# Moving half blocks, row selections, mask slices and transposes to other steps of an image

## The reference

```python
om = conv(x, w_om, 3x3) + b_om             # 108 channels: 36 dy, 36 dx, 36 mask
py = h - 1 + ki + dy ; px = w - 1 + kj + dx  # per group (4), tap (9), pixel
v  = (bilinear sample of x at py, px, zero outside) * sigmoid(mask)
out = relu(einsum('ogck,bgckhw->bohw', w_dcn, v)) + x
```

## Time and profile before

| what | us |
|---|---|
| median of 3 runs | 207.06 |
| the runs | 206.66 to 207.31 |
| the profiled execution | 207.24 |
| its span, first to last instruction | 205.1 |
| busy in the span: PE / PEld | 180.4 / 127.2 |
| busy in the span: DVE / ACT / POOL | 161.3 / 106.3 / 86.2 |

### The profile page before, as it was taken

How to read it: one execution, slowest core, us unless ns; L and a number is a source line. 1 busy time by engine, 2 the same in 40 slices (tenths; PEclk the granted TensorE clock), 3 DMA queues, 4 the chain that set the end, 5 groups by cost and what they waited for, 6 DMA issues and landing times.

```text
span 205.1 us, 4582 instructions
## 1 busy us (share of the span) xinstructions
PE 180.4 (88%) x1806; PEld 127.2 (62%) x1806; DVE 161.3 (79%) x268; ACT 106.3 (52%) x199; POOL 86.2 (42%) x103
## 2 busy tenths in 40 slices
PE   0398997979899989999889999999969999998980
PEld 0234944644356544477578779639958789877870
DVE  0899778994768859887889779717999798899922
ACT  1146057500007784688748757836766687864000
POOL 8237952864013096504444344240661554442000
PEclk9999999999999999999999999999999999999999
DMA  6940000000130000010011000000002000000000
GB/s 189 327 33 2 3 0 0 3 0 0 29 77 19 20 27 9 25 36 3 9 36 25 0 3 0 3 0 3 9 25 70 20 2 16 0 16 2 19 0 21
DMA packets 8499, 5.54 MB, mean 27 GB/s; under 512 B 4887, under 2 KB 7461, under 8 KB 8473
## 3 DMA queue, kind: packets, MB, share of 16 engines
q1 hardware_dynamic: 8089, 4.25, 8.1%
q10 hardware_dynamic: 288, 0.89, 1.4%
q0 software_dynamic: 96, 0.06, 0.1%
HBM read 2.82 MB, written 0.52 MB: 16 GB/s over the span
## 4 chain that ended last, share of the span: by engine, by line
PE 66%; DVE 16%; ACT 6%; issue 4%; DMA 3%; POOL 2%; SPq 0%; DVEq 0%; ACTq 0%; POOLq 0%
PE ps L1254 20%; PE ps L1228 10%; PE ps L1148 10%; PE ps L1044 4%; PE ps L1165 3%; DVE smp_prod L777 3%; DMA x_parts<-in_x 3%; PE ps L1296 3%; PE ps L1302 3%; PE ps L1081 3%; PE ps L1213 2%; PE ps L1199 2%; DVE smp_prod L888 2%; PE ps L1182 2%; DVE windows_attention L873 1%
## 5 line engine op out<-in xcount | busy, mean ns | idle before, releaser
L888 DVE TENSOR_TENSOR smp_prod<-ps,hx_selx 128x768 f32<-128x768 f32 x72 | 67.5, 953 | 10.1 <-PE ps L1228 8.8
L1254 PE MATMUL ps<-smp_prod,windows_attention 128*64 128x192 f32 (+2 forms) x512 | 54.9, 336 | 0.0
L1254 PEld LDWEIGHTS ps<-smp_prod,windows_attention 128*64 128x64 f32 x512 | 40.1, 136 | 4.1 <-ACT windows_attention L575 0.3
L1228 PE MATMUL ps<-haty,by_rows 128*64 128x256 f16 x432 | 39.4, 275 | 2.0 <-DVE smp_prod L888 1.8
L451 POOL TENSOR_SCALAR disty<-disty 64x512 f32<-64x512 f32 (+1 forms) x23 | 13.5, 586 | 64.3 <-ACT haty L596 64.2
L1228 PEld LDWEIGHTS ps<-haty,by_rows 128*64 128x64 f16 x432 | 26.1, 109 | 9.7 <-DVE smp_prod L888 3.9
L604 ACT ACTIVATE hx_selx<-ps 128x512 f32<-128x512 f32 x36 | 21.3, 591 | 10.8 <-PE ps L1213 10.8
L458 POOL TENSOR_TENSOR haty<-disty,haty 64x512 f16<-64x512 f32 (+1 forms) x23 | 24.0, 1042 | 1.9
L1148 PE MATMUL ps<-conv_staged 128*108 128x512 f32 (+1 forms) x60 | 23.3, 521 | 0.7 <-ACT x_parts L568 0.7
L606 ACT ACTIVATE hx_selx<-hx_selx 128x512 f32<-128x512 f32 x36 | 22.7, 631 | 1.2
L591 ACT ACTIVATE disty<-ps 128x512 f32<-128x512 f32 (+1 forms) x24 | 12.5, 521 | 12.3 <-PE ps L1199 12.3
...
## 6 DMA issues: line engine op xcount, KB each, us to landing
...
```

The lines of the kernel that those rows point to most:

```text
L888: nc.vector.tensor_tensor(pairs, rows, cols.unsqueeze(1).to_broadcast([P, QUARTERS, HW]), ALU.mult).then_inc(s_mult, 1)
L1228: ins = nc.tensor.matmul(ps[h * C:(h + 1) * C, at:at + HW], by_matrix(a, QUARTERS - 1 - k)[:, h * C:(h + 1) * C], haty[i % 2][:, p * HW:(p ...
L1254: return nc.tensor.matmul(dst[:, at:at + strips * 3 * SP].rearrange("p (s k n) -> p s k n", k=3, n=SP), rows, sampled(i, ki, m, first, str ...
```

## The change

Half block (1,1) stays at step 0, (2,0) goes from step 1 to 2 and (2,1) from 2 to 3. The row selections go from steps 1, 3, 7 to 2, 6, 8, the mask slices from 0, 2, 6, 8 to 0, 3, 5, 7 (in image 0 from 4, 5, 6, 8 to 4, 5, 7, and in image 1 there are five instead of four). VectorE's last values of an image go from step 3 to 4. Images 1 and 2 transpose at steps 2, 3, 5 instead of 2, 3, 4, 5, and image 3 gets two groups, at steps 2 and 3; VectorE copies a group out of bank 4 in the same step and not in the next. The waits for copied groups ahead of blocks and `final` name other groups accordingly.

```diff
--- before.py
+++ after.py
@@ -64,9 +64,9 @@
 YW, YP = [HW, 2 * HW, 2 * HW], [0, 1, 3]
 MSLOT = 3 * BANK + 3 * HW
 
-MASKS = [{4: (0, 0), 5: (0, 1), 6: (0, 2), 8: (0, 3)}, {0: (0, 4), 2: (0, 5), 6: (1, 0), 8: (1, 1)},
-         {0: (1, 2), 2: (1, 3), 6: (1, 4), 8: (1, 5)}, {0: (2, 0), 2: (2, 1), 6: (2, 2), 8: (2, 3)},
-         {0: (2, 4), 2: (2, 5)}, {0: (3, 0), 2: (3, 1), 6: (3, 2), 8: (3, 3)}, {0: (3, 4), 2: (3, 5)}, {}]
+MASKS = [{4: (0, 0), 5: (0, 1), 7: (0, 2)}, {0: (0, 3), 1: (0, 4), 3: (0, 5), 5: (1, 0), 7: (1, 1)},
+         {0: (1, 2), 3: (1, 3), 5: (1, 4), 7: (1, 5)}, {0: (2, 0), 3: (2, 1), 5: (2, 2), 7: (2, 3)},
+         {0: (2, 4), 3: (2, 5)}, {0: (3, 0), 3: (3, 1), 5: (3, 2), 7: (3, 3)}, {0: (3, 4), 3: (3, 5)}, {}]
 
 
 PIECES = [(0, 0, HW), (0, HW, BANK), (1, 0, BANK), (2, 0, BANK), (3, 0, BANK)]
@@ -74,16 +74,16 @@
 CONV_BANK = [4, 0, 6, 6, 4]
 EARLY = 3
 PAIRS_AT = {(0, m): (EARLY + m, 4) for m in range(6)} | {
-    (1, 2): (9, 6), (1, 3): (10, 6), (1, 4): (11, 4), (1, 5): (12, 4),
-    (2, 2): (13, 6), (2, 3): (14, 6), (2, 4): (15, 4), (2, 5): (16, 4)}
+    (1, 2): (9, 6), (1, 3): (10, 6), (1, 5): (11, 4), (2, 2): (12, 6), (2, 3): (13, 6), (2, 5): (14, 4),
+    (3, 2): (15, 6), (3, 3): (16, 6)}
 PARTS_AT = {(0, m + 1): (2, m) for m in range(5)} | {(1, m + 2): (3, m) for m in range(5)} | {(4, m): (4, m) for m in range(5)}
 STAGE_AT = {(0, 0): 1, (0, 2): 2, (0, 7): 3}
 LAST_CONV = 3
 FAR = 5
 CHUNK, VALS, SLICES = 3, 3, 6
-SEL_Y = {1: 0, 3: 1, 7: 2}
+SEL_Y = {2: 0, 6: 1, 8: 2}
 BLOCKS = {6: (0, 0), 7: (0, 1), 8: (1, 0)}
-LATE = {0: (1, 1), 1: (2, 0), 2: (2, 1)}
+LATE = {0: (1, 1), 2: (2, 0), 3: (2, 1)}
 FINAL = 5
 
 
@@ -937,16 +937,17 @@
                         values(i, 0, it)
                     if m == 1 and i:
                         values(i - 1, 1, it)
-                    if m == 3 and i:
+                    if m == 4 and i:
                         values(i - 1, 2, it)
                     if m == FINAL + 1 and i:
                         accumulate(i - 1, it)
                         if isinstance(it, int):
                             finish(i - 1, 1)
                     if isinstance(it, int):
-                        if (i, m - 1) in PAIRS_AT:
-                            g, src = PAIRS_AT[i, m - 1]
-                            if g % 2:
+
+                        for at in (m - 1, m):
+                            g, src = PAIRS_AT.get((i, at), (0, 0))
+                            if g % 2 and (at == m) == (i > 0 and src == 4):
                                 window_out(g, it, src)
                         if (i, m) in PARTS_AT:
                             offset_part(*PARTS_AT[i, m])
@@ -1331,7 +1332,7 @@
                                          stop=True).then_inc(s_amaxT, 1)
                     if m in BLOCKS:
                         if i < 3 and m == 6 and isinstance(it, int):
-                            windows_out(8 + 4 * i, it)
+                            windows_out(8 + 3 * i, it)
                         if i == 0 and m == 8 and isinstance(it, int):
                             pe.wait_ge(s_omraw, 4)
                         if (i, m) == (LAST_CONV, 6) and isinstance(it, int):
@@ -1356,7 +1357,7 @@
                         spread_mask(*MASKS[i][m], it)
                     if (i, m) in PAIRS_AT and isinstance(it, int):
                         g, dst = PAIRS_AT[i, m]
-                        if i == 0 or m in (3, 5):
+                        if i == 0 or m == 3:
                             windows_out(g - 1, it)
                         else:
                             pe.wait_ge(s_vals, VALS * (i - 1) + (2 if m == 2 else 3))
@@ -1364,12 +1365,12 @@
                             pe.wait_ge(s_staged, {4: 2, 8: 3, 12: 4}[g])
                         windows(g, it, dst)
                     if m == FINAL and i:
-                        if i in (1, 2) and isinstance(it, int):
-                            windows_out(6 + 4 * i, it)
+                        if i in (1, 2, 3) and isinstance(it, int):
+                            windows_out(7 + 3 * i, it)
                         if i == FAR and isinstance(it, int):
                             pe.wait_ge(s_choice, 1)
                         final(i - 1, it)
-                for m in range(3):
+                for m in LATE:
                     block_of_products(B - 1, *LATE[m], it)
                 final(B - 1, it)
```

## The result

The changed kernel takes **204.23 us** (median of four runs, 203.85 to 204.55); the kernel before took 207.19 us beside it on the same chip (206.66 to 207.38). The ratio is 0.9855, with a 95% interval of 0.9833 to 0.9877: 2.96 us or 1.45% faster. The forecast was 205.0 us with a range of 203.4 to 206.8. The profiled execution took 204.55 us, its span 202.5 us, so a difference of spans (2.6 us) is what the two traces have to explain. Of the runs of the experiments one is left out of the medians and ratios as a slow one, over 1.5% above the fastest of its kernel (213.30 us, all but the half blocks).

A forecast was written before the change was run, and what follows sets the result against it. Late stretches were taken as bound by VectorE and TensorE together, neither filling them, stretch 3 by TensorE alone. Terms -1.5 +0.4 +0.1 -0.5 -0.6 = -2.1 us gave 205.0 us, range 203.4 to 206.8.

The forecast's parts named there:

- stretch 7: Last sampling-loop stretch, cut at final projections: alternating heavy and light steps removes TensorE waits; worked out 0.80 us gain, 0.6 taken.
- stretches 1 and 2: Sampling-loop stretches with transposes: fewer groups and no waits for VectorE copies, less 0.2 for mask slice 2; -1.5 us.
- stretch 3: TensorE-bound sampling-loop stretch: two transpose groups come (0.84 us), the 0.40 us wait at bank 7 goes; +0.4 us.
- stretches 4 and 5: Sampling-loop stretches: VectorE's work on the last offsets in image 4 stays, values come one step later; +0.1 us.
- stretch 6: Sampling-loop stretch like the last but with mask slices: the 0.64 us wait for bank 7 goes; -0.5 us.
- the sentence on the Trainium skill: GpSimd contends with two-SBUF-input VectorE instructions; moved chain keeps full speed, result copy loses its GpSimd neighbour; gains 0.8 us in stretch 7.
- alternation: Sampling-loop steps: light steps between heavy ones cut VectorE and TensorE waits; worked out on stretch 7, 0.80 us gain.
- Slice 2 at step 7: Mask slice 2 moves to one step before the values that read it; hidden if TensorE is late there, 0.2 us charged.
- (a): Rival, more gain than counted: VectorE's idle falls to 0.6 us in stretches 1, 2, 4 to 7; 203.5 us, chance 0.10.
- (b): Rival, waits only move: 0.2 us more before the final projection in seven images, 0.3 for slice 2; 206.7 us, chance 0.12.
- (c): Rival, second row selection's ScalarE and GpSimd chain makes step 1's broadcast late: 3.9 us over seven images, 208.9 us, chance 0.08.
- (d): Rival, TensorE pauses at lone light steps halve the clock for one stretch, costing several us; chance 0.02.

## Why the prediction was right

Sign and size hold, and so does the mechanism of stretch 7: 205.0 was forecast, 204.23 measured, -2.1 us against -3.0. That the total came out is in part luck: too much was expected of the transposes and too little of the rest, and two terms are at or over their bounds. Term by term, from the starts of the final projections:

| term | forecast | bounds | measured |
|---|---|---|---|
| stretches 1 and 2 | -1.5 | -2.7 to -0.6 | -2.4 |
| stretch 3 | +0.4 | 0 to +1.0 | +1.16 |
| stretches 4 and 5 | +0.1 | -1.0 to +0.8 | -0.07 |
| stretch 6 | -0.5 | -0.9 to 0 | -0.89 |
| stretch 7 | -0.6 | -0.8 to -0.2 | -0.62 |

**Stretch 7, the table of steps.** The working had TensorE's steps at 1.58, 1.30, 1.77, 1.22, 0.55, 1.29, 1.44 and the final projection 10.16 us after step 6 (189.17-179.01). Measured: 1.58, 1.30, 1.75, 1.36, 0.54, 1.31, and 187.13-176.96 = 10.17 us. The table's 0.80 came (10.96 before, 10.17 now). It shows as 0.62 in the stretch since from the projection's start to step 6 it is now 176.96-175.49 = 1.47 us instead of 1.30; the projection that has waited for values no longer has its weights loaded ahead (they were 0.11 ahead, at 177.60). That I took 0.6 and not the table's 0.8 was for another reason, the copy that stayed slow, which did not happen; so this term was right by chance in its last 0.2. For the slow copy the prediction had a gain of 0.2 to 0.4; the run with the half blocks alone, where it took 1.03, has 0.51. The sum of the table is right to 0.01, its steps are off by up to 0.14 (step 0: 1.22 worked out, 1.36 measured). The wait for values before the projection, 0.2 in the table, is 0.27.

**The result copy at line 921.** The step behind the sentence on the Trainium skill (GPSIMD Engine Reference, Specifications) held, and the trace agrees: VectorE's copy lost its GpSimd neighbour and takes 0.42 in all eight. But the moved chains got other neighbours. Two casts now stand beside one and take 0.79 and 1.11 us (82.43 and 142.88), 0.41 and 0.42 before, which the prediction didn't count.

**Stretch 6** gained 0.89, at its far bound, 0.24 of it the slice that crossed the border. The wait for bank 7 did not go as claimed: 0.32 us is left at 169.51, and 0.32 at 142.53. The sentence "row selections at 2, 6, 8 and slices at 0, 3, 5, 7 leave step 4 between" overlooked that 7 and 8 stand next to each other, as do 5 and 6. The test "selections waiting under 0.2 us" fails with it. So of the 0.64 us the term rested on, half came; the rest of the gain I put down to TensorE's light steps, which no longer stand in a row (VectorE's idle falls from 1.40 us to 0.82).

**Stretches 1 and 2, and 3.** The transposes were to be worth -1.5 and +0.4. Stretch 0, left as it is, is as before to 0.03. All four waits on copies did go, as the prediction's test asked (none over 0.5; the longest pause 0.33). But the run with the transposes alone shows that they only move time: -1.27, +0.20, +1.09. Two steps failed in stretch 3. One is the price of a group: I put 0.42, its weight loads; from its first weight load to the next instruction it takes 0.59 us (126.99 to 127.58), with up to 0.33 of idle weight loading ahead, and both groups stand in stretch 3, where TensorE has no idle to hide them (19.58 of 19.58). Between the changed kernel and the one without the transposes stretch 3 differs by 1.23, so a group is 0.6. The other is the 0.40 at bank 7: it did go, but in the kernel without the transposes the stretch is only 0.07 shorter, since the convolution waits 0.37 for the later values. 1.23 less 0.07 is the 1.16. And of the 2.4 us that stretches 1 and 2 gained, 0.76 are there without the transposes, by the half blocks and the new tables, which the prediction did not count there.

**The sum, by parts.** The prediction had 1.1 us of net gain in the transposes and 1.0 in the rest. The runs have 0.6 and 2.4. So the total was nearer than its parts, which is luck. What it missed is that alternation needs the selections out of step 3 to gain anything over the whole kernel: it was worked out on stretch 7, "where neither transposes nor masks disturb", and the half blocks do gain 0.51 alone there; in stretch 6 they gain 0.24 alone and 0.65 with the tables, the slice not counted.

**Slice 2 at step 7.** Charged 0.2; VectorE waits 1.45 us for it at 93.30. It was a cover that held, since stretch 1 is TensorE's (13.25 of 13.32 busy). The kernel with the tables alone shows the same nearness uncovered, for the last slice: 2.77 us of TensorE and a halved clock, +5.4 us. The prediction did not see that the two moves, slice and values, hold each other up.

**The rivals.** (a), more than counted, went half way: stretches 1, 2, 6 did better, stretch 3 worse. (b), waits only move, is out: before the final projections of stretches 4 and 7 TensorE waits 0.21 and 0.27 us for values, no more than in the table. (c) did not come but is one step away: "just in time", with 185.0 against 184.88, is some 0.1 us of margin in the trace (182.81 against weight loads from 182.92), and the selection one step later costs 5.4 us. It was right to give it a price, and its size (3.9) was of the right order. (d): the granted clock is 1.00 in every stretch, with waits up to 1.12 us at 150.23. What the prediction could not see from its one trace is that the kernel before was 2 us longer in five of 45 executions, at its lowest mean clocks; the changed one wasn't in its four. The warning of the Trainium skill (TensorE: Matmul & The Clock Gate, section on psum-queue depth-cycling) doesn't bear on the changed kernel; in the kernel with the tables alone the clock did fall, once after a single long wait, and once after three us of short pauses; the second is the case of the warning. What made that one fall is open.
